# The first layer's messages in a two-layer graph network: the edge MLP taken two groups ahead on ScalarE, and each group's node rows copied to a fixed buffer

## The reference

```
Wxh  = x @ Wl.T + bl
h    = silu(rbf @ Wf1.T + bf1)
f_ij = h @ Wf2.T + bf2
msg  = f_ij * Wxh[j]                      # one row of 64 per edge
agg  = segment_sum(msg, i, num_segments=12500)
```

## Time and profile before

| | |
|---|---|
| median of 3 runs | 4693.3 us |
| profiled execution, its own time | 4689.24 us |
| span of its trace, first to last instruction | 4687.5 us |
| PE busy | 2535.9 us (54%) |
| PEld busy | 2071.5 us (44%) |
| DVE busy | 2643.0 us (56%) |
| ACT busy | 887.9 us (19%) |
| POOL busy | 2384.9 us (51%) |

### The profile page before, as it was taken

One profiled execution on the slowest core, in us unless ns is written; L12 is line 12 of the kernel. 1 busy time (PEld: TensorE's weight loads), 2 busy tenths in 40 slices (PEclk: granted clock), 3 DMA queues, 4 the chain that ended last, 5 costly groups with the idle time before them and its releaser, 6 DMA issues. The chain is left out here.

```text
span 4687.5 us, 81175 instructions
## 1 busy us (share of the span) xinstructions
PE 2535.9 (54%) x28074; PEld 2071.5 (44%) x28075; DVE 2643.0 (56%) x5354; ACT 887.9 (19%) x1671; POOL 2384.9 (51%) x2228
## 2 busy tenths in 40 slices
PE   3556556655555556555555655637514433435775
PEld 2444444444444444444444444436513333334764
DVE  5555555555545455555555555546674544445776
ACT  2111111111111111111111111101133333331002
POOL 0456656566655656566566666621263333333552
PEclk9767667667767677776777777669855555557998
DMA  7322222222222222222222222248715555557993
GB/s 211 86 65 69 65 62 71 63 65 70 64 63 63 65 62 69 64 64 67 67 64 64 70 66 68 59 163 331 271 45 190 180 190 179 186 184 286 400 398 127
DMA packets 205906, 585.25 MB, mean 125 GB/s; under 512 B 57272, under 2 KB 74432, under 8 KB 193216
## 3 DMA queue, kind: packets, MB, share of 16 engines
q1 hardware_dynamic: 134016, 369.03, 25.7%
q0 software_dynamic: 68336, 213.37, 12.5%
q10 hardware_dynamic: 3408, 0.92, 0.1%
HBM read 389.22 MB, written 194.13 MB: 124 GB/s over the span
## 5 line engine op out<-in xcount | busy, mean ns | idle before, releaser
L1019 POOL DMA_INDIRECT region_rows<-x_space,pos x1664 | 1793.3, 1078 | 1151.5 <-DVE x_space L972 632.5
L886 PEld LDWEIGHTS ps_fx<-tmp_space,window 128*128 128x128 bf16 x9984 | 483.9, 117 | 526.6 <-issue 523.8
L972 DVE TENSOR_TENSOR x_space<-rest,x_space 128x512 bf16<-128x512 f32 x208 | 144.0, 692 | 971.3 <-issue 572.2
L868 PE MATMUL ps_rank<-onehot,tri 128*128 128x98 bf16 x1664 | 160.9, 266 | 919.0 <-DVE onehot L907 913.9
L886 PE MATMUL ps_fx<-tmp_space,window 128*128 x9984 | 521.8, 219 | 237.5 <-issue 235.2
L868 PEld LDWEIGHTS ps_rank<-onehot,tri 128*128 128x128 bf16 x1664 | 119.0, 128 | 981.4 <-DVE onehot L907 975.8
L880 PE MATMUL ps_th<-in_t,w_wf 128*128 128x512 f32 x416 | 424.1, 1123 | 0.0
L1336 PE MATMUL ps_th<-tmp_space,x_space 128*128 128x64 bf16 x2646 | 158.8, 242 | 477.2 <-DVE x_space L1300 477.2
L1336 PEld LDWEIGHTS ps_th<-tmp_space,x_space 128*128 128x128 bf16 x2646 | 143.5, 131 | 492.4 <-DVE x_space L1300 492.4
L823 ACT ACTIVATE hid_t<-ps_th,w_bf 128x512 f32<-128x512 f32 x208 | 142.9, 687 | 1121.5 <-PE ps_th L880 542.4
L1372 POOL TENSOR_TENSOR agg<-x_space,agg 128x576 f32<-128x576 f32 x131 | 178.4, 1362 | 344.2 <-ACT agg L1352 344.2
(11 more groups left out here) (232 smaller groups left out, 4834.4 us busy)
## 6 DMA issues: line engine op xcount, KB each, us to landing
tmp_space<-region_rows SPq DMA_DIRECT2D x98, 882.0 KB, 6.5
run_rows<-agg SPq DMA_DIRECT2D x98, 873.0 KB
x_space<-key_rows SPq DMA_DIRECT2D x98, 576.0 KB
x_space<-rbf SPq DMA_DIRECT2D x208, 256.0 KB
rel_bc<-rel_rows SPq DMA_DIRECT2D x208, 256.0 KB
region_rows<-x_space,pos POOLq DMA_INDIRECT x1664
region_rows<-x_space SPq DMA_DIRECT2D x1, 14259.0 KB, 73.1
wxh_rows<-agg POOLq DMA_DIRECT2D x1, 3328.0 KB, 23.3
```

Source lines behind the costliest of these rows:

```text
L868: e.matmul(ps_rank[:, 0:NB], tri[:, :], onehot[j % 2][:, t, :], start=(t == 0), stop=(t == T - 1))
L886: last = e.matmul(ps_x[:, t * D:(t + 1) * D], window_t[:, h, t * P:(t + 1) * P], wxh[:, bass.ds(b + h, 1), c, :].rearrange("p b d -> p (b ...
L972: e.tensor_tensor(rows_b[j][:, :, 2 * D:3 * D], left, rows_b[j][:, :, D:2 * D], ALU.subtract).then_inc(lw, 1)
L1019: e.indirect_dma_start(out=region_rows, out_offset=bass.IndirectOffsetOnAxis(ap=pos[j][:, t:t + 1], axis=0), in_=rows_f[j][:, t, :], in_of ...
```

## The change

ScalarE's program gets a new helper `nearby`, which for the group two ahead reads `base_i`, copies the two blocks' rows of `wxh` (384 bf16 values per partition) to one of two fixed buffers `near`, and copies the group's 16 values of `ind` to `sides`. TensorE's gather matmuls and its third set of counting matmuls read these buffers, so that their addresses no longer come from a register. ScalarE's order becomes: high and middle part of this group, then `nearby`, `inputs` and `hidden` of the group two ahead. On TensorE the transposes of the next group stand behind the gather matmuls, and the next group's hidden-layer matmul behind the filter's. On VectorE the bias addition becomes a helper of its own (`filters`), called where it stood before.

```diff
                 @block.scalar
-                    def steady(i, j):
-                        after(inputs, i, j)
+                    def nearby(i, j):
+                        b = e.value_load(base_i[0:1, bass.ds(i * S + j, 1)], min_val=0, max_val=NB - 1)
+                        e.wait_ge(xw, count_of(i, j, 2))
+                        e.copy(near[j % 2], wxh[:, bass.ds(b, 2), :, :].rearrange("p b c d -> p (b c d)")).then_inc(nr, 1)
+                        e.wait_ge(rk, count_of(i, j, 2))
+                        e.copy(sides[j % 2], ind[:, tiles(i, j), :]).then_inc(sd, 1)
+                    def parts(i, j):
                         high_part(i, j)
-                        after(hidden, i, j)
                         middle_part(i, j)
...
+                    with e.Fori(0, passes - 1) as i:
+                        for j in range(S):
+                            parts(i, j)
+                            after(nearby, i, j, 2)
+                            after(inputs, i, j, 2)
+                            after(hidden, i, j, 2)
                 @block.tensor
+                    def blocks(i, j, b):
...
+                        e.wait_ge(sd, count_of(i, j))
+                        for t in range(T):
+                            last = e.matmul(ps_pairs[0:NB, bass.ds(b, 2)], onehot[j % 2][:, t, :], sides[j % 2][:, t, :],
+                                            start=False, stop=False)
+                        last.then_inc(rk, 1)
+                    def nodes(i, j):
+                        e.wait_ge(nr, count_of(i, j))
+                        e.wait_ge(m, count_of(i, j, 1))
+                        e.wait_ge(wi, count_of(i, j))
...
+                                        near[j % 2][:, (h * PARTS + c) * D:(h * PARTS + c + 1) * D],
...
+                    def steady(i, j, ahead):
+                        b = e.value_load(base_i[0:1, bass.ds(i * S + j, 1)], min_val=0, max_val=NB - 1)
+                        blocks(i, j, b)
+                        nodes(i, j)
+                        if ahead:
+                            after(inputs, i, j)
+                        outputs(i, j)
+                        if ahead:
+                            after(hidden, i, j)
                 @block.vector
-                    def products(i, j):
+                    def filters(i, j):
                         e.wait_ge(m, count_of(i, j, 1))
                         e.wait_ge(f2, count_of(i, j))
                         e.tensor_tensor(f_s[:, :, :], ps_f[:, :].rearrange("p (t d) -> p t d", d=D),
                                         wts["bf2"][:, None, :].broadcast_to([P, T, D]), ALU.add).then_inc(f1, 1)
+                    def products(i, j):
...
                         after(positions, i, j)
+                        after(filters, i, j)
```

More of the change, by code:

```diff
@@ L775, in sorted_messages @@
             rbf_s, msg = found[S:2 * S], found[2 * S:2 * S + 2]
+            near = [a.bitcast(BF16) for a in found[2 * S + 2:2 * S + 4]]
+            sides = [a.bitcast(BF16).rearrange("p (t k) -> p t k", k=2) for a in found[2 * S + 4:2 * S + 6]]
             left = rest[:, :].rearrange("p (t d) -> p t d", d=D)
@@ L786, in sorted_messages, with after @@
             gate = only_if(sorted_i, True)
-            def after(body, i, j):
-                body(i + (j + 1) // S, (j + 1) % S)
+            def after(body, i, j, by=1):
+                body(i + (j + by) // S, (j + by) % S)
             with nc.Block() as block:
@@ new lines, in inputs, with hidden @@
+                    def inputs(i, j):
+                        e.wait_ge(ld[j], i * 16 + 16)
+                        e.wait_ge(ev, count_of(i, j, 1))
+                        for t in range(T // 2):
+                            last = e.transpose(ps_t[:, t * P:(t + 1) * P],
+                                               rbf_s[j][:, t * P:(t + 1) * P], ident[:, :])
+                        last.then_inc(tr, 1)
+                    def hidden(i, j):
+                        e.wait_ge(si, count_of(i, j, 1))
+                        e.wait_ge(ev, count_of(i, j))
+                        e.matmul(ps_h[:, :], wts["wf1"][:, :], in_t[:, :], start=True, stop=True).then_inc(h1, 1)
@@ new lines, in nodes @@
+                    def nodes(i, j):
+                        e.wait_ge(nr, count_of(i, j))
+                        e.wait_ge(m, count_of(i, j, 1))
+                        e.wait_ge(wi, count_of(i, j))
+                        for t in range(T):
+                            for h in range(2):
+                                for c in range(PARTS):
+                                    last = e.matmul(
+                                        ps_x[:, t * D:(t + 1) * D], window_t[:, h, t * P:(t + 1) * P],
+                                        near[j % 2][:, (h * PARTS + c) * D:(h * PARTS + c + 1) * D],
+                                        start=(h == 0 and c == 0), stop=(h == 1 and c == PARTS - 1))
+                        last.then_inc(xw, 1)
@@ new lines, in outputs @@
+                    def outputs(i, j):
+                        e.wait_ge(f1, count_of(i, j, 1))
+                        e.wait_ge(si, count_of(i, j))
+                        for t in range(T // 2):
+                            last = e.matmul(ps_f[:, t * P:(t + 1) * P], hid_t[:, t * P:(t + 1) * P],
+                                            wts["wf2"][:, :], start=True, stop=True)
+                        last.then_inc(f2, 1)
+                    def steady(i, j, ahead):
[7 more added lines that the diff above has]
+                            after(hidden, i, j)
@@ L897, in _ @@
+                    inputs(0, 0)
+                    hidden(0, 0)
+                    with e.Fori(0, passes - 1) as i:
+                        for j in range(S):
+                            steady(i, j, True)
+                    for j in range(S):
+                        steady(passes - 1, j, j + 1 < S)
                     e.matmul(ps_pairs[0:NB, 0:NBP], zeros[:, 0:NB], zeros[:, 0:NBP], start=False, stop=True).then_inc(f_zero, 1)
```

73 lines of the change are left out of this document (22 added, 51 removed).

## The result

The changed kernel takes 4953.99 us (median of 4 runs, 4951.49 to 4962.97), the kernel before 4686.36 us beside it (4 runs): a ratio of 1.0577, 95% interval 1.0547 to 1.0607. The profiled execution has a span of 4950.1 us against 4687.5, 262.6 us more. The forecast was 4830 us: the direction and the alternation came, 124 us of the size did not.

The account below looks back on a forecast made before the run. A ring held by ScalarE's Silu bounds the kernel, GpSimd's DMAs next, with TensorE's results held in long runs. Terms sum to 29.6 us per two groups, 3064 us against 2920, +144: 4830 us, range 4310 to 4940.

Parts of the forecast that it names:

- The middle part: On ScalarE, ahead of the Silu, it lets the low part start 3.80 us after the multiplication instead of 8.44.
- The copies cost nothing: On ScalarE, two copies and a register load, at most 1.6 us, fit beside other work; taken as 0.
- GpSimd's gap of 0.30 us, and the alternation: GpSimd idles 0.30 and about 8 us in turn; multiplication steps alternate between about 9 and 20 us.
- The sum of the cycle: Two groups of the changed stage take 29.6 us, 14.8 a group; over 207 steps +144 us.
- the bias addition starts when GpSimd ends: 0 to 2.5 us after; I take 2.0: On VectorE, the bias addition of group k+2 waits for the end of GpSimd's two-group run; 2.0 us taken.
- my ends: Cycle limits: 27.4 us, 4605 us; or 31.5 us, about 5030, with 1.1 us late filter and 0.8 us late Silu.
- its likeliest case: Alternating stalls in the changed stage: 4830 us, own range 4700 to 4930, chance 0.56.
- within 2.5 us of POOL's last DMA: Sign: in every second group the bias addition waits some 8 to 11 us, ending that soon after GpSimd's last DMA.
- POOL-bound: Rival: stalls were chance or go with the order; GpSimd sets 11.2 us a group, 4096 us; chance 0.14.
- Self-regulating: Rival: mild TensorE delay in each group gives GpSimd its pause; 12.3 us a group, 4322 us; chance 0.14.
- Three groups a run: Rival: TensorE's filter gets through early, GpSimd runs three groups in a row; 13.4 us a group, 4535 us; chance 0.09.
- No net change: Rival: a two-group cycle of 28.2 us, bias addition only 0.6 us after GpSimd's end; 4690 us; chance 0.07.

Follow-up runs that it names:

- two memsets: Changed kernel with two idle memsets for GpSimd ahead of each group's scatter: 4424.94 us, 0.9447 of the kernel before.
- a third of the gathers: Changed kernel with one of three bf16 parts of wxh gathered, 16 matmuls a group in place of 48: 4638.52 us; on another chip 4049.8 us.
- no rows: Changed kernel with every row's position out of range, so GpSimd issues DMAs but writes no row: 15.22 us a group; on another chip 10.91.
- 4 memsets: Changed kernel with four idle memsets for GpSimd ahead of each group's scatter: 4585.48 us, ratio 0.9797; on another chip 4535.79 us, ratio 1.0787.
- turns: Changed kernel with GpSimd waiting, ahead of a group's scatter, for the next group's filter matmuls: 4815.48 us, 1.03 of the kernel before.
- the middle part's place alone: Kernel before with one line moved, ScalarE's middle part ahead of the next group's Silu: 4887.33 us, 1.0439 of the kernel before.

## Why the prediction was right or wrong, point by point

**The middle part.** Right: 3.65 us from multiplication to low part in the undisturbed groups (3.80 predicted), the undisturbed step 9.1 us (8.65, or 9 to 9.5 with a slow clock: the gathers above took 2.44 us at a granted clock of 0.60, those of the earlier trace rows 1.94 us at 0.79).

**The copies cost nothing.** Right: 0.51 and 0.20 us each, and 4928 us without them.

**GpSimd's gap of 0.30 us, and the alternation.** Right, in kind: gaps of 0.30 and about 9.4 us in turn (0.30 and 8.15 predicted), steps of 9.1 and 21.6 us.

**The sum of the cycle.** Here it failed. Medians of the 97 cycles that I could take apart, against the terms:

| term | predicted | measured |
|---|---|---|
| multiplication to low part | 3.80 | 4.25 |
| to GpSimd's start | 1.58 | 1.59 |
| first run | 10.93 | 11.03 |
| gap | 0.30 | 0.30 |
| second run | 10.2 | 9.97 |
| GpSimd's end to the bias addition | 2.0 | 2.78 |
| to the multiplication | 0.77 | 0.73 |
| sum, two groups | 29.6 | 30.65 |

1.05 us a cycle over 103.5 cycles are 109 us of the 113 by which the measured 3177 us exceed the 3064 of the sum; 6 us lie outside the stage. Two terms carry it. The step "the bias addition starts when GpSimd ends: 0 to 2.5 us after; I take 2.0" was mis-sized: I took the wait's end as a release of finished work throughout. Of 101 cycles counted by this, in 21 the filter's matmuls had all started before GpSimd's end, and there the forecast came true, 2.12 us in the median against my 2.0. In the other 80 TensorE isn't done, and it is 2.93 us. In the timeline at 1500 us six of the eight filter matmuls start after GpSimd's end at 1527.47, in two pieces, and are done at 1530.3. And the low part is late in the first group of each pair, because the late filter makes the hidden layer late, the Silu L832 waits for it (1501.91 in the timeline, after 2.22 us) and the high part and with it the rest L1009 stand behind (after the late results of the timeline at 2868 us it is ScalarE's late copy L827 that the hidden layer L881 waits for). Both stood among my ends, at 1.1 and 0.8 us, more than the 0.78 and 0.45 us that came, and were left out of the sum. That the late filter is behind both is read from timelines; no run parts them. The sign "within 2.5 us of POOL's last DMA" missed with it.

**The range.** 4310 to 4940 missed 4954 by 14 us. Its upper end was set well below the 5030 that the prediction itself named as the far end of its likeliest case.

**The rivals.** POOL-bound, 4096 us: this is what happens on a free chip, 4053 us without the copies. So the rule of the Trainium skill behind it ("SBUF — State Buffer", section "SBUF: two separate sides"), by which TensorE waits for no one, agrees with the free chips (not one slow step in over 60,000 gathers). On the holding ones the time that I drew from it doesn't come; whether it is for SBUF that TensorE is late there no run shows. Self-regulating, 4322 us: not reached by itself, but two memsets of pause come to 4425. Three groups a run: none of the 104 runs of the result's trace, 6 of the 101 in the trace of the same kernel on another holding chip. No net change: not seen.

## What to carry to other kernels

An engine that reaches its result earlier also starts its successor earlier; look for what the successor's idle gap was paying for before closing it. Where a trace shows a stall that no semaphore explains, count it by the state of the other engines (here GpSimd's gap before the group): a change that brings every other group into that state makes the kernel slower. And a gain that hangs on such a stall is measured on more than one chip, and at more than one time, before it is believed, since here its sign turned.

## What the runs showed of the hardware

**While GpSimd issues indirect DMAs, TensorE is slowed and its results come late, on some chips.** On a free chip no group shows either form. For the second form see the counts above: all 22 long steps of the kernel before, 64 of 64 with a third of the gathers, 22 of 103 and 78 of 100 in two traces of the changed kernel. For the first, from all gather matmuls of the stage I took the time from one start to the next within a group, sorted by how long GpSimd had been issuing without a gap of over 0.5 us; in brackets the share of steps over 0.3 us, which are mostly about 0.7 us long.

| kernel, chip | GpSimd idle over 1 us | 3 to 6 us | 6 to 8 us | 8 to 11 us | over 11 us |
|---|---|---|---|---|---|
| changed, holding | 0.038 us (0%) | few | 0.069 (3%) | 0.246 (29%) | 0.467 (47%) |
| no rows, holding | 0.039 (0%) | 0.068 (3%) | 0.067 (3%) | 0.203 (24%) | 0.410 (39%) |
| 4 memsets, holding | 0.052 (0%) | 0.087 (7%) | 0.195 (21%) | 0.298 (31%) | few |
| turns, holding | 0.048 (0%) | 0.136 (14%) | 0.241 (28%) | 0.243 (26%) | none |
| 4 memsets, free | few | 0.051 (0%) | 0.050 (0%) | 0.051 (0%) | none |
| no rows, free | none | none | few | few | 0.044 (0%) |

**A count or a time?** The first slow gather of a run comes, in the median, 3.5 us after GpSimd's start in the kernel with turns, 5.3 with four memsets, 6.7 with two, 8.2 in the changed kernel and 10.2 in the kernel before. TensorE had started 47, 54, 59, 55 and 63 matmuls by then. The times differ by a factor of 2.9, the counts by 1.3. That looks like a stock that GpSimd's idle time refills (1.90 us are enough, 0.30 us are not) and its issuing doesn't. Two kernels speak against it: with the middle part's place alone it is 84 matmuls at 9.7 us, with a third of the gathers 95 at 19.0 us; and results that come late after finished matmuls are not explained by a stock of matmuls. So this is a guess. The Trainium skill ("Advanced Engine Details and Errata", section "Engine Queue Depths") gives TensorE a queue of 64 instructions; that the stock is this queue, no run here shows.

**What makes a chip hold or be free stays open.** GpSimd's issues (1058 and 1070 ns), the packets and bytes, and the other stages look alike in the two traces of the kernel without copies. The kernel before was not profiled on a free chip, so where its 480 us go there is argued only. The span outside this stage is 1764 to 1808 us in every profiled run but those without rows, on chips of either kind, so they should lie in this stage: an estimate of 11.6 us a group there, where it is 14.1 on a holding chip.
